# Edge offsets of a graph kernel: a second copy in bf16, stored in reading order

## The chip, the cores and the metric

The kernel runs on one core of one Trainium2 chip. The metric is the device time of one execution in microseconds, as the median of several runs. The engines are TensorE (PE, with its weight loads as PEld), VectorE (DVE), ScalarE (ACT), GpSimd (POOL) and SyncE (SP, which here only issues DMAs).

## What is computed

A graph of N = 6250 nodes with 128 features and E = 200000 edges, sorted by destination. First one attention layer (GAT) with 4 heads, a residual and a layer norm; then three message-passing layers with a gate per edge, and a last residual and layer norm.

```
xh = (x @ W).reshape(-1, H, C)                      # GAT
alpha = leaky_relu((xh[dst]*a_i).sum(-1) + (xh[src]*a_j).sum(-1), 0.2)
ex = exp(alpha - segment_max(alpha, dst)[dst])
out = segment_sum(xh[src] * ex / segment_sum(ex, dst)[dst], dst)
...
for l in range(3):                                  # message passing
    hk = relu(concat([h[dst], h[src]]) @ linA_w[l].T + linA_b[l])
    w = sigmoid(hk @ linB_w[l].T + linB_b[l])
    prop = segment_sum(w * h[src], dst)
    emb = relu(concat([h, prop]) @ lin_w[l].T + lin_b[l])
```

## The kernel before

The edges are worked in NG = 392 groups of GE = 512. Within a group, edge p*4 + t (T = 4) lies in partition p, column t. Since the edges are sorted, the destinations of a group nearly always lie in a window of W = 32 nodes that begins at the group's `base`; the rare further windows have a loop of their own (`extra_windows`), which finds nothing to do with these inputs.

For each group four things are made ready:
- **The source rows.** GpSimd gathers one table row of 1 KB for each edge, with four indirect DMAs of 128 rows for a group (`gather`, L572, the issue is L579). The tables are `gat_rows` for GAT and `mp_rows` for a layer. The target `G` has U = 8 slots; from the ninth group on a gather waits until the group eight earlier has been used up (`R` in GAT, `agg` in a layer). The row numbers are copied to `idx` by ScalarE (L654) some four groups ahead.
- **The window.** SyncE loads the offsets of the group's 512 edges from `REL` in DRAM, broadcast to 128 partitions (GAT, L477) or 96 (a layer, L532), into a ring of four slots `relbc`, and the window's own rows (`sm` or `awin`). An offset is destination minus base.
- **The one-hot `sel`,** edges in partitions, 32 nodes in columns (L965).
- **The transposed one-hot `selT`,** nodes in partitions, 512 edges in columns, in bf16. `make_selT` (L968, the operation is L969) compares the broadcast offsets with the partition's node number. The offsets lie in edge order (p, t); TensorE takes 128 edges of one t as weights, so the result is written in the order (t, p): the read runs through, the write goes from one t to the next at a stride of 128 elements of 2 bytes. It is used as weights in L1523 (GAT) and L1636 (a layer).

Each engine works through a software pipeline written out by hand: on VectorE in the order `gat_order` or `mp_order`, where the first number is how many groups a stage lags. Per step of a layer these are hidden (L1341, one group behind, waits for the gathered rows), the sum into `acc` (L1371), the transposed one-hot (L969), logits (L1352), the weighted one-hot (L1360) and `sel` (L965). In GAT the transposed one-hot comes between the maximum of the group before (L996) and the product `R` (L1105, the gathered rows by the exponentials, both in SBUF). Two short casts (L1013, L1022) round to bf16 there. `rhs` (L1035) is VectorE's last result before TensorE's L1523. Loops run over turns of eight groups; VectorE loads the bases of a turn into registers at its start (L1147).

Ahead of it all, VectorE prepares the lists: L884 makes the offsets `relF` (98 partitions of 2048), L887 casts the sources, L893 copies TensorE's transposes of both lists, and up to L914 follow small steps. The semaphore `prep` counts these. SyncE stores `REL` (L443) after L884; GpSimd fills `acc` (L569) when all are done and `REL` is stored, since the lists lie in the same memory. Then come the GAT table (SyncE L455) and the first gathers.

Of the kernel before, what the change touches and what calls it, by code (L numbers as in the profile page):

```python
# [16 lines left out]
BF16 = mybir.dt.bfloat16  # L17
ALU = mybir.AluOpType
# [3 lines left out]
T = 4  # L22
GE = P * T
W = 32
# [21 lines left out]
PREP_SRC = PREP_REL + 1  # L46
# [44 lines left out]
def gnn_kernel(nc, x, src, dst, W0, att, linA_w, linA_b, linB_w, linB_b, lin_w, lin_b, gamma, beta, final_w, final_b,  # L91
# [20 lines left out]
    PADDST = 16 * N  # L112

# [5 lines left out]
    REL = nc.dram_tensor("rel_dst", (NG, GE), F32, kind="Internal").ap()  # L119
    MORE = nc.dram_tensor("more_windows", (1, NG), I32, kind="Internal").ap()  # L120
    BASE = nc.dram_tensor("window_base", (1, NG), I32, kind="Internal").ap()

    with ExitStack() as ctx:
# [18 lines left out]
        relF = mh[0:QP, 0:QW]  # L142

# [19 lines left out]
        relbc = ring[:, 0:4, :]  # L163
# [99 lines left out]
        rel_stored = sem("rel_stored")  # L263
        base_stored = sem("base_stored")
# [145 lines left out]
        def _(sp):  # L410
# [32 lines left out]
            sp.dma_start(REL.rearrange("(q c) e -> q (c e)", c=CQ), relF).then_inc(rel_stored, 16)  # L443
            sp.wait_ge(base_stored, 16)
# [24 lines left out]
            sp.wait_ge(rel_stored, 16)  # L469
            sp.wait_ge(pads_stored, 32)  # L470
            sp.wait_ge(si_out, 16 * NT)

            def gat_window(k0, off):
                base = sp.value_load(base_sb[0:1, bass.ds(k0 + off, 1)], min_val=0, max_val=N - 1)
                if reached(k0, off, 4):
                    sp.wait_ge(gat["rhs"], k0 + (off - 3))
                sp.dma_start(relbc[:, off % 4, :], REL[bass.ds(k0 + off, 1), :].rearrange("o e -> (o e)")  # L477
                             .partition_broadcast(P)).then_inc(win_in[off % 4], 16)
                sp.dma_start(sm[:, off % 4, 0, 0:1], SI[bass.ds(base * H, W * H), :]).then_inc(win_in[off % 4], 16)
# [7 lines left out]
            with extra_windows(sp, 0) as at:  # L487
                sp.wait_ge(x_free, at.w + (at.q + 1))
                sp.sem_inc(waited, 1)
                sp.dma_start(relbc[:, 0, :], REL[bass.ds(at.g, 1), :].rearrange("o e -> (o e)")  # L490
                             .partition_broadcast(P)).then_inc(x_win, 16)
                sp.dma_start(sm[:, 0, 0, 0:1], SI[bass.ds(at.node * H, W * H), :]).then_inc(x_win, 16)
# [12 lines left out]
            with sp.Fori(0, L) as l:  # L505
# [22 lines left out]
                def window(k0, off):  # L528
# [3 lines left out]
                    sp.dma_start(relbc[0:S * W, off % 4, :], REL[bass.ds(k0 + off, 1), :].rearrange("o e -> (o e)")  # L532
# [11 lines left out]
                with extra_windows(sp, l + 1) as at:  # L544
                    sp.wait_ge(x_free, at.w + (at.q + 1))
                    sp.sem_inc(waited, 1)
                    sp.dma_start(relbc[0:S * W, 0, :], REL[bass.ds(at.g, 1), :].rearrange("o e -> (o e)")
                                 .partition_broadcast(S * W)).then_inc(x_win, 16)
                    sp.dma_start(awin[:, 0, :],
                                 A3[bass.ds(at.node, W), :].rearrange("n (s d) -> (n s) d", s=S)).then_inc(x_win, 16)  # L550
# [12 lines left out]
        def _(pool):  # L563
# [4 lines left out]
            pool.wait_ge(rel_stored, 16)  # L568
            nc.gpsimd.memset(acc[:, :, :], 0.0).then_inc(acc_cleared, 1)  # L569
# [269 lines left out]
        def _(dve):  # L839
# [46 lines left out]
            assert done[0] == PREP_REL  # L886
            then(v.tensor_copy(srcF, srcI))  # L887
# [80 lines left out]
            def make_selT(k0, off, tile, rows, node, made):  # L968
                v.tensor_scalar(tile[0:rows, off % 4, :].rearrange("n (t p) -> n p t", t=T),  # L969
                                relbc[0:rows, off % 4, :].rearrange("n (p t) -> n p t", t=T),  # L970
                                node, None, ALU.is_equal).then_inc(made, 1)
# [182 lines left out]
            def make_extra_sel(at, tile, rows, node, selT_done, sel_done, window):  # L1154
# [8 lines left out]
                                relbc[0:rows, 0, :].rearrange("n (p t) -> n p t", t=T),  # L1163
# [558 lines left out]
```

## Time and profile before

| what | value |
|---|---|
| median of 3 runs | 9366.73 us (9366.05 to 9370.35) |
| span of the profiled execution | 9351.7 us |
| GpSimd busy | 6739.1 us (72%) |
| VectorE busy | 6023.4 us (64%) |
| TensorE busy | 4974.9 us (53%) |
| ScalarE busy | 1410.9 us (15%) |
| gathers in GAT, L579 | 1568, 1779.5 us |
| gathers in the layers, L579 | 4704, 4920.1 us |
| transposed one-hot, L969 | 1568, 2178.9 us |
| DMA engines, share of the span | gathers 30.2%, queue of SyncE and ScalarE 15.6% |

The profile is of one execution, whose own time is not listed among the runs; its span is from the first to the last instruction. A busy time is the sum of an engine's instructions without register and semaphore work. A busy engine need not be the one that sets the time: that is read from the chain that ended last and from what each instruction waited for. TensorE is granted half of its full clock nearly throughout (0.515 on the mean).

### The profile page before, as it was taken

How to read it: one execution, taken by the hardware profiler on the slowest of the kernel's cores; microseconds unless marked ns; L12 is line 12 of the kernel's file. 1: busy time of each engine (PE TensorE's matmuls, PEld its weight loads, DVE VectorE, ACT ScalarE, POOL GpSimd, SP SyncE). 2: the span in 40 equal slices, each digit the busy share in tenths (PEclk: the TensorE clock that was granted, in tenths of full speed). 3: DMA queues.
4: the chain of work that ended last, by engine and by line, in shares of the span. 5: the costliest groups of instructions: out<-in, count | busy, mean ns of one | idle time of the engine just before them, and what ended most of it. 6: DMA issues, size and time to landing. Idle time of an engine off the chain costs nothing.

```text
span 9351.7 us, 148690 instructions
## 1 busy us (share of the span) xinstructions
PE 4974.9 (53%) x27078; PEld 4220.6 (45%) x27079; DVE 6023.4 (64%) x26793; ACT 1410.9 (15%) x5406; POOL 6739.1 (72%) x6331
## 2 busy tenths in 40 slices
PE   2777777777744444444454444444445444444445
PEld 1666666666633333333343333333334333333334
DVE  4888888888856555555556555655555555555656
ACT  1222222222410000000020000000002000000002
POOL 1777777777457777777746777777773777777774
PEclk7555555555555555555565555555556555555555
DMA  2444444444344444444434444444443444444443
GB/s 81 138 137 138 138 138 137 137 138 138 92 137 138 138 138 138 138 138 137 138 109 133 139 138 138 139 138 138 138 135 108 139 137 138 139 138 139 138 139 100
DMA packets 752005, 1241.72 MB, mean 133 GB/s; under 512 B 323315, under 2 KB 387641, under 8 KB 751419
## 3 DMA queue, kind: packets, MB, share of 16 engines
q0 software_dynamic: 301056, 822.48, 30.2%
q1 hardware_dynamic: 444380, 413.53, 15.6%
q10 hardware_dynamic: 6275, 3.20, 0.1%
q14 instruction: 283, 2.32, 0.1%
q8 instruction: 11, 0.18, 0.0%
HBM read 1194.48 MB, written 44.13 MB: 132 GB/s over the span
## 4 chain that ended last, share of the span: by engine, by line
POOL 54%; issue 24%; DMA 6%; DVE 5%; PE 5%; SPq 2%; DVEq 1%; POOLq 1%; ACT 0%; ACTq 0%
POOL G L579 54%; DMA G<-mp_rows,idx 3%; DMA G<-gat_rows,idx 2%; PE ps L1646 2%; DVE junk L1352 1%; SPq L520 1%; PE ps L1551 1%; SPq L513 1%; DMA gat_rows<-ring 1%; DMA mp_rows<-acc 0%; PE ps L1511 0%; DVEq L957 0%; SPq L414 0%; DMA mp_dst_rows<-acc 0%; PE ps L1676 0%
## 5 line engine op out<-in xcount | busy, mean ns | idle before, releaser
L579 POOL DMA_INDIRECT G<-mp_rows,idx x4704 | 4920.1, 1046 | 1810.7 <-issue 1391.1
L1646 PE MATMUL ps<-selw,G 128*128 128x32 f32 x9408 | 2222.2, 400 | 468.8 <-DVE selw L1360 462.9
L1646 PEld LDWEIGHTS ps<-selw,G 128*128 128x128 f32 x9408 | 2093.9, 327 | 751.2 <-issue 652.3
L1341 DVE TENSOR_TENSOR pen<-ps,G 128x512 f32<-128x512 f32 x1176 | 813.1, 691 | 2502.2 <-DMA G<-mp_rows,idx 2500.0
L1636 PE MATMUL ps<-awin,ring 96*128 96x128 bf16 x4704 | 714.5, 307 | 2986.2 <-DVE ring L969 2986.2
L969 DVE TENSOR_SCALAR ring<-ring,pF 96x512 bf16<-96x512 f32 (+1 forms) x1568 | 2178.9, 1390 | 2.5 <-DMA sm<-gat_si 2.1
L579 POOL DMA_INDIRECT G<-gat_rows,idx x1568 | 1779.5, 1135 | 552.7 <-issue 526.5
L1636 PEld LDWEIGHTS ps<-awin,ring 96*128 96x128 bf16 x4704 | 404.2, 130 | 3142.9 <-DVE ring L969 3142.9
L1352 DVE SCALAR_TENSOR_TENSOR junk<-pen,cur 128x128 f32<-128x128 f32 x4704 | 1282.3, 328 | 0.1
L787 ACT ACTIVATE gate<-logit,cur 128x4 f32<-128x4 f32 x1176 | 349.6, 297 | 5870.5 <-DVE junk L1352 5263.8
L1551 PE MATMUL ps<-sel,weighted 128*128 128x32 f32 x3136 | 750.7, 404 | 0.0
L1551 PEld LDWEIGHTS ps<-sel,weighted 128*128 128x128 f32 x3136 | 698.0, 327 | 25.3
L1511 PE MATMUL ps<-ident,G 128*128 128x128 f32 x1568 | 428.7, 429 | 345.3 <-DMA G<-gat_rows,idx 344.9
L666 ACT ACTIVATE pen<-ring,negbig 128x512 f32<-128x512 bf16 x392 | 282.9, 722 | 1518.8 <-DVE ring L969 1518.8
L965 DVE TENSOR_TENSOR sel<-iotaF,rel_all 128x128 f32<-128x128 f32 x1568 | 449.6, 287 | 13.0 <-issue 11.6
L996 DVE CUSTOM_DVE_ANT_0 junk<-ps,pen 128x512 f32<-128x512 f32 x392 | 268.7, 685 | 291.0 <-issue 240.9
L1511 PEld LDWEIGHTS ps<-ident,G 128*128 128x128 f32 x1568 | 280.6, 217 | 363.6 <-issue 236.7
L1352 DVE DVE_READ_ACCUMULATOR junk<-pen,cur 128x1 f32 x4704 | 378.8, 81 | 0.0
L1360 DVE TENSOR_TENSOR selw<-sel,gate 128x128 f32<-128x128 f32 x1176 | 334.6, 285 | 0.2
L654 ACT COPY idx<-idx_all 128x4 int32 (+1 forms) x1572 | 284.3, 182 | 40.7 <-issue 40.6
L1105 DVE TENSOR_TENSOR weighted<-G,weighted 128x512 f32<-128x512 f32 x392 | 270.9, 691 | 0.0
L1523 PE MATMUL ps<-rhs,ring 128*128 128x24 bf16 x1568 | 106.6, 184 | 281.4 <-DVE rhs L1035 281.3
(176 smaller groups left out, 5146.1 us busy)
## 6 DMA issues: line engine op xcount, KB each, us to landing
ring<-rel_dst SPq DMA_DIRECT2D x1176, 192.0 KB
ring<-rel_dst SPq DMA_DIRECT2D x392, 256.0 KB
G<-mp_rows,idx POOLq DMA_INDIRECT x4704
awin<-mp_dst_rows SPq DMA_DIRECT2D x1176, 24.0 KB
G<-gat_rows,idx POOLq DMA_INDIRECT x1568
mp_rows<-acc SPq DMA_DIRECT2D x30, 625.0 KB
mp_dst_rows<-acc SPq DMA_DIRECT2D x30, 468.8 KB
sm<-gat_si SPq DMA_DIRECT2D x392, 0.5 KB
```

The source lines that it names most:

```text
L579: pool.indirect_dma_start(out=G[:, u, width * t:width * (t + 1)], out_offset=None, in_=table, in_offset=bass.IndirectOffsetOnAxis(ap=idx[: ...
L654: nc.scalar.copy(idx[:, T * (off % U):T * (off % U) + T], idx_all[:, bass.ds(k0 * T + off * T, T)]).then_inc(idx_ready, 1)
L787: nc.scalar.activation(gate[:, off % 4, :], logit[:, off % 4, :], ACT.Sigmoid, bias=cur[:, C_BB:C_BB + 1]).then_inc(done["gate"], 1)
L965: v.tensor_tensor(sel[:, off % U, :].rearrange("p (t n) -> p t n", t=T), iotaW, rel4, ALU.is_equal).then_inc(made, 1)
L969: v.tensor_scalar(tile[0:rows, off % 4, :].rearrange("n (t p) -> n p t", t=T), relbc[0:rows, off % 4, :].rearrange("n (p t) -> n p t", t=T ...
L1341: v.tensor_tensor(pen[:, off % 2, :].rearrange("p (t c) -> p t c", t=T), PS[off % 2][:, :].rearrange("p (t c) -> p t c", t=T), Grows[:, of ...
L1352: v.scalar_tensor_tensor(junk[:, P * t:P * t + P], pen[:, off % 2, P * t:P * t + P], 0.0, cur[:, C_B:C_B + D], ALU.max, ALU.mult, accum_ou ...
L1360: v.tensor_tensor(selw[:, off % 4, :].rearrange("p (t n) -> p t n", t=T), sel[:, off % U, :].rearrange("p (t n) -> p t n", t=T), gate[:, o ...
L1511: i = tr(PS[off % 2][:, P * t:P * t + P], Grows[:, off % U, t, D:2 * D], ident[:, :])
L1551: i = mm(PS[4 + b][:, 0:W], R[:, b, D * t:D * t + D], sel[:, off % U, W * t:W * t + W], start=(t == 0), stop=(t == T - 1))
L1636: i = mm(PS[off % 2][:, D * t:D * t + D], selT16[0:S * W, off % 4, P * t:P * t + P], awin[:, off % 4, :], start=True, stop=True)
L1646: i = mm(PS[2 + off % 2][:, 0:W], Grows[:, off % U, t, 0:D], selw[:, off % 4, W * t:W * t + W], start=(t == 0), stop=(t == T - 1))
```

## The change

The offsets are stored a second time, in `REL16`, as bf16 and in the order (t, p). One VectorE operation on the 98x2048 offsets makes them, between the making of `relF` and the cast of the sources; it also limits them to 255, which changes no comparison with 0 to 31 and keeps what is stored a whole number that bf16 holds exactly. SyncE stores them, and waits for that store before the first window; so does GpSimd before it fills `acc`. The window loads of both stages read `REL16`. `make_selT` compares with unit stride on both sides, bf16 in and out. The loops over further windows go on with `REL` in fp32.

```diff
+    NONE16 = 255.0
+    REL16 = nc.dram_tensor("rel_dst16", (NG, GE), BF16, kind="Internal").ap()
+        rel16 = acc[0:QP, 0, 2 * QW:3 * QW].bitcast(BF16)[:, 0:QW]
-        relbc = ring[:, 0:4, :]
+        relbc = ring[:, 0, :]
+        relbc16 = ring[:, 0:4, :].bitcast(BF16)[:, :, 0:GE]
...
             sp.dma_start(REL.rearrange("(q c) e -> q (c e)", c=CQ), relF).then_inc(rel_stored, 16)
+            sp.wait_ge(prep, PREP_REL16)
+            sp.dma_start(REL16.rearrange("(q c) e -> q (c e)", c=CQ), rel16).then_inc(rel16_stored, 16)
...
+            sp.wait_ge(rel16_stored, 16)
...
-                sp.dma_start(relbc[:, off % 4, :], REL[bass.ds(k0 + off, 1), :].rearrange("o e -> (o e)")
+                sp.dma_start(relbc16[:, off % 4, :], REL16[bass.ds(k0 + off, 1), :].rearrange("o e -> (o e)")
...
-                    sp.dma_start(relbc[0:S * W, off % 4, :], REL[bass.ds(k0 + off, 1), :].rearrange("o e -> (o e)")
+                    sp.dma_start(relbc16[0:S * W, off % 4, :], REL16[bass.ds(k0 + off, 1), :].rearrange("o e -> (o e)")
...
             pool.wait_ge(rel_stored, 16)
+            pool.wait_ge(rel16_stored, 16)
...
+            then(v.tensor_single_scalar(rel16.rearrange("q (c t p) -> q c p t", c=CQ, t=T),
+                                        relF.rearrange("q (c p t) -> q c p t", c=CQ, t=T), NONE16, ALU.min))
+            assert done[0] == PREP_REL16
             then(v.tensor_copy(srcF, srcI))
...
             def make_selT(k0, off, tile, rows, node, made):
-                v.tensor_scalar(tile[0:rows, off % 4, :].rearrange("n (t p) -> n p t", t=T),
-                                relbc[0:rows, off % 4, :].rearrange("n (p t) -> n p t", t=T),
-                                node, None, ALU.is_equal).then_inc(made, 1)
+                v.tensor_scalar(tile[0:rows, off % 4, :], relbc16[0:rows, off % 4, :], node, None,
+                                ALU.is_equal).then_inc(made, 1)
```

No instruction changes its place; one is added on VectorE and one DMA on SyncE. VectorE's preparation before, where the names are output<-input:

```order
L884 TENSOR_TENSOR mh<-acc,baseF 98x2048
L887 CAST acc<-acc 98x2048
L893 COPY rel_all<-ps 128x4x98 x4
L893 CAST idx_all<-ps 128x4x98 x4
L895 COPY idx_all<-idx_all 128x16
```

The same place in the changed kernel:

```order
L894 TENSOR_TENSOR mh<-acc,baseF 98x2048
L897 TENSOR_SCALAR acc<-mh 98x4x128x4
L900 CAST acc<-acc 98x2048
L906 COPY rel_all<-ps 128x4x98 x4
L906 CAST idx_all<-ps 128x4x98 x4
L908 COPY idx_all<-idx_all 128x16
```

The new operation (L897) stands ahead of the cast of the sources, so all that follows on VectorE comes after it.

## Rows read from the trace of the kernel before

**Rows 1.** the page's part 4, shares of the chain that ended last, by line
```profile
POOL G L579 54%; DMA G<-mp_rows,idx 3%; DMA G<-gat_rows,idx 2%; PE ps L1646 2%; DVE junk L1352 1%; SPq L520 1%; PE ps L1551 1%; SPq L513 1%; DMA gat_rows<-ring 1%; DMA mp_rows<-acc 0%; PE ps L1511 0%; DVEq L957 0%; SPq L414 0%; DMA mp_dst_rows<-acc 0%; PE ps L1676 0%
```

**Rows 2.** L579 by stretch: length, busy us (x count), granted clock, DMA share, GB/s
```profile
196.50:2453.40 2256.90, 1779.48 (x1568) 0.50 0.49 138
2605.00:4761.80 2156.80, 1643.69 (x1568) 0.50 0.48 138
4864.20:7016.70 2152.50, 1639.14 (x1568) 0.50 0.48 138
7117.70:9268.30 2150.60, 1637.18 (x1568) 0.50 0.48 138
sum 8716.80, POOL 6699.49; mean POOL 1674.87
```

**Rows 3.** single lines: ns min/median/max, first to last start, forms; then its wait
```profile
L969 DVE TENSOR_SCALAR ring<-ring,pF x1568: 1347/1357/1604, 203.7 to 9265.5; 96x512 bf16<-96x512 f32 x147, 128x512 bf16<-128x512 f32 x49
...
  DMA sm<-gat_si: 2.1, 1
...
L579 POOL DMA_INDIRECT G<-mp_rows,idx x4704: 942/947/1943, 2605.0 to 9267.3; - x196
...
L1299 DVE TENSOR_SCALAR ring<-mh x150: 210/221/440, 2573.0 to 7148.4; 128x125 f32 x90, 128x125 f32<-128x125 f32 x60
```

**Rows 4.** timeline, message passing: start us, us, engine, line, [idle before]
```profile
5500.60 0.69 DVE L1341 TENSOR_TENSOR pen<-ps,G 128x512 f32<-128x512 f32 x1 [2.97 <-DMA G<-mp_rows,idx]
5500.85 1.93 POOL L579 DMA_INDIRECT G<-mp_rows,idx  x1 [0.30 <-issue]
...
5501.30 1.35 DVE L969 TENSOR_SCALAR ring<-ring,pF 96x512 bf16<-96x512 f32 x1
...
5506.83 0.95 POOL L579 DMA_INDIRECT G<-mp_rows,idx  x1 [0.30 <-issue]
...
5507.58 1.36 DVE L969 TENSOR_SCALAR ring<-ring,pF 96x512 bf16<-96x512 f32 x1
```

**Rows 5.** timeline, GAT: short VectorE operations beside gathers
```profile
644.35 0.69 DVE L1105 TENSOR_TENSOR weighted<-G,weighted 128x512 f32<-128x512 f32 x1
644.55 1.32 POOL L579 DMA_INDIRECT G<-gat_rows,idx  x1 [0.30 <-issue]
...
1223.55 1.05 POOL L579 DMA_INDIRECT G<-gat_rows,idx  x1 [0.30 <-issue]
...
1223.78 0.17 DVE L1022 CAST sm<-sm 128x2 bf16<-128x2 f32 x1
```

**Rows 6.** timeline, GpSimd: first gather without L969, first with, last with, last without
```profile
196.46 1.10 POOL L579 DMA_INDIRECT G<-gat_rows,idx  x1 [75.30 <-issue]
...
203.01 0.95 POOL L579 DMA_INDIRECT G<-gat_rows,idx  x1 [0.30 <-issue]
...
9265.55 1.46 POOL L579 DMA_INDIRECT G<-mp_rows,idx  x1 [0.30 <-issue]
9267.31 0.95 POOL L579 DMA_INDIRECT G<-mp_rows,idx  x1 [0.30 <-issue]
```

**Rows 7.** timeline, GAT: VectorE's pause, then TensorE from group to group
```profile
1220.30 0.69 DVE L996 CUSTOM_DVE_ANT_0 junk<-ps,pen 128x512 f32<-128x512 f32 x1 [5.82 <-issue]
...
1224.99 0.26 PE L1523 MATMUL ps<-rhs,ring 128*128 128x24 bf16 x4 [3.86 <-DVE rhs L1035]
...
1229.68 0.26 PE L1523 MATMUL ps<-rhs,ring 128*128 128x24 bf16 x4 [0.48 <-DVE rhs L1035]
...
1234.24 0.26 PE L1523 MATMUL ps<-rhs,ring 128*128 128x24 bf16 x4 [0.35 <-DVE rhs L1035]
```

**Rows 8.** timeline, start: VectorE's cast, its next copy, GpSimd's fill
```profile
82.77 1.23 DVE L887 CAST acc<-acc 98x2048 f32<-98x2048 int32 x1
90.48 3.42 DVE L893 COPY rel_all<-ps 128x392 f32<-128x392 f32 x4 [6.48 <-PE ps L1481]
...
104.98 10.76 POOL L569 MEMSET acc<- 128x12800 f32 x1 [103.73 <-DVE moreI L914]
```

More of the change, by code:

```diff
@@ L45 @@
 PREP_REL = PREP_CONST + 5
-PREP_SRC = PREP_REL + 1
+PREP_REL16 = PREP_REL + 1
+PREP_SRC = PREP_REL16 + 1
 PREP_IDX = PREP_SRC + 2 * T + 1
@@ L263, in gnn_kernel @@
         rel_stored = sem("rel_stored")
+        rel16_stored = sem("rel16_stored")
         base_stored = sem("base_stored")
@@ L489, in _ @@
                 sp.sem_inc(waited, 1)
-                sp.dma_start(relbc[:, 0, :], REL[bass.ds(at.g, 1), :].rearrange("o e -> (o e)")
+                sp.dma_start(relbc, REL[bass.ds(at.g, 1), :].rearrange("o e -> (o e)")
                              .partition_broadcast(P)).then_inc(x_win, 16)
@@ L546, in _ @@
                     sp.sem_inc(waited, 1)
-                    sp.dma_start(relbc[0:S * W, 0, :], REL[bass.ds(at.g, 1), :].rearrange("o e -> (o e)")
+                    sp.dma_start(relbc[0:S * W, :], REL[bass.ds(at.g, 1), :].rearrange("o e -> (o e)")
                                  .partition_broadcast(S * W)).then_inc(x_win, 16)
@@ L1162, in make_extra_sel @@
                 v.tensor_scalar(tile[0:rows, 0, :].rearrange("n (t p) -> n p t", t=T),
-                                relbc[0:rows, 0, :].rearrange("n (p t) -> n p t", t=T),
+                                relbc[0:rows, :].rearrange("n (p t) -> n p t", t=T),
                                 shift[0:rows, 0:1], node, ALU.subtract, ALU.is_equal).then_inc(selT_done, 1)
```

## The prediction

> **What bounds the kernel now.** I read the views in this order. The chain that ended last comes first: more than half of it is GpSimd issuing gathers on one line [rows 1]. Then that line alone, in the four stretches in which gathers run, the GAT pass and three message-passing layers: each stretch has 1568 of them, and together the stretches are 8716.8 us of the 9351.7 us span [rows 2]. So outside the stretches lie only 634.9 us, and the time of the kernel is above all the number of gathers times the pitch of one. The reader is to see in the timeline what a pitch is: a gather of 0.95 us, then 0.30 us of issue, with no wait for a buffer or a result [rows 4]. Nothing on GpSimd stands between two gathers, so only the length of a gather can change its pace.
>
> That length varies. In the message-passing layers its median is 947 ns, its minimum 942 ns, its maximum 1943 ns [rows 3]. 6272 gathers of 0.947 us would be 5939.6 us; the profile has 6699.5 [rows 2]. The excess is 759.9 us.
>
> Where does it come from? Laying GpSimd beside VectorE shows it. In the message-passing stage a gather that starts at 5500.85 lasts 1.93 us; the transposed one-hot (L969) starts 0.45 us after it and ends at 5502.65, and the gather ends 0.13 us later. One turn on, the same VectorE operation starts 0.75 us into a gather, and that gather takes its usual 0.95 us [rows 4]. So GpSimd stands still in the middle of a gather until L969 has ended. I did this for all 6272: 2213 gathers have L969 running somewhere in their span, and they hold 721.3 us of the excess; the other 4059 hold 38.7 us. The first and the last gather of the two sets are in [rows 6]. The 38.7 us belong to other VectorE work: a gather with a two-input product at its start takes 1.32 us [rows 5].
>
> The Trainium skill (SBUF — State Buffer, "SBUF: two separate sides") has the mechanism: VectorE and GpSimd share a pair of ports, and a VectorE operation in a two-port mode keeps GpSimd from writing descriptors; the next section of that page has it blocked until about 115 ns after the operation's end. The 0.13 us above agrees. The page also speaks against this change: a bf16 operation of unit stride is in its faster two-port mode, so it would still lock.
>
> **The change part by part.** *The one-hot itself.* There are 1176 + 392 = 1568 of them, each 1.36 us now for 512 elements [rows 3]. That is 2.65 ns an element, while a two-input fp32 product over 512 elements needs 0.69 us [rows 5]; what L969 has and the product has not is an output scattered over 2-byte elements at a stride of 128. The change makes input and output bf16 and contiguous. The trace has no such operation. The bounds are the nearest rows: 0.22 us for a one-input fp32 operation over 125 elements [rows 3] from below, and the 0.69 us of the product from above. I take 0.3 us: the product has two inputs, and the form is nearer to the one-input row. The Trainium skill (VectorE: DVE Perf Modes, "Side-by-side") would give (150 + 8 + 128) cycles at 0.96 GHz, an estimate of 0.30 us for the new form; for the old one it would allow two elements a cycle, some 0.43 us, and the measured 1.36 us decides against that.
>
> VectorE itself gains nothing for the time by this, since it waits for gathers. What counts is how much of the 721.3 us stays. What a short one does, the trace shows with a cast of 0.17 us (L1022), by the same engine and with one input: of 390 casts placed clear of L969, 44 started 0.2 to 0.3 us after a gather and cost it 0.10 us, as at 1223.55 [rows 5]; 53 cost some 0.01 us and the others nothing. That is 0.01 us each. A 0.3 us operation covers the sensitive places (the start of the gather, which the product at 644.35 hits, and about 0.25 us in) twice as often, and for about 0.15 us longer. In GAT, L969 starts 0.1 to 0.3 us after a gather's start in 130 of 392 cases, at some 0.15 to 0.2 us each: 22 us. In message passing 1130 of 1176 start later than 0.45 us after a gather's start, where that gather takes no harm [rows 4]; 536 of these start in the last 0.3 us before the next gather and can reach into its start. Half of them at some 0.06 us are 15 us. Together 37 us stay, between 0 (all fall free) and 130 us (0.25 us for a third of 1568). The term is -721 + 37 = **-684 us**.
>
> *The loads.* The broadcast of the offsets moves half the bytes, 1568 times. Nobody waits for these loads: the only wait for the window is a single one, at the first group [rows 3]. Zero; the cover is that a load is issued about three groups ahead, and if it were gone the load would still be shorter than before.
>
> *The preparation.* A 98x2048 operation is added on VectorE between L884 and L887, in the scattered form on its output. At L969's 2.65 ns an element it takes 5.4 us; contiguous it would be the 1.23 us of the cast behind it [rows 8]. That cast now starts at 82.77 and ends at 84.00; the next instruction starts at 90.48, after 6.48 us of idleness until TensorE's transposes [rows 8]. With 5.4 us more the cast ends at 89.4, still before 90.48. Taken at 0, at most 1 us. Behind the new wait on SyncE stand the load of the bases and the stores of the pads, and on GpSimd the fill of `acc`, which starts at 104.98 after 103.7 us of idleness that the end of VectorE's preparation sets [rows 8]; the store issued at about 88 has 16 us to land. Zero.
>
> *What is late next.* At 1.25 us a gather, a group is 5.0 us of GpSimd. In message passing VectorE has 3 us to spare, spent waiting for gathers [rows 4]. In GAT less is to spare: when gathers are there in time, TensorE takes 4.69 and 4.56 us from one group to the next, of which 0.48 and 0.35 us are waiting for VectorE, so 4.2 us of its own [rows 7]. And once in a turn of eight groups VectorE stands for 5.8 us, which TensorE sees as a wait of 3.9 us [rows 7]. The turn is now 2256.9 / 49 = 46.1 us. As they are, those two would allow 8 x 4.6 + 5.8 = 42.6 us; with L969 1 us shorter the waits of 0.35 to 0.48 us go, and it is 8 x 4.2 + 3.9 = 37.5. GpSimd needs 8 x 4 x 1.25 = 40.0. So GpSimd stays the bound, by 2.5 us of 40, and what is late next is again the gather.
>
> **Sum.** The profiled execution has a span of 9351.7 us and becomes 9351.7 - 684 = 8667.7 us. The median of the runs, 9366.7, lies 15.0 us above the span, for what is around it: 9366.7 - 684 = **8683 us**.
>
> **Rivals.**
> *In proportion (10%).* The blocking may not fall away below a certain length but shrink with it. Now each L969 costs 721 / 1568 = 0.46 us of a possible 1.36 + 0.12 = 1.48, or 31%. At the same share an operation of 0.3 us costs 0.13 us and one of 0.69 us costs 0.25 us: 204 or 394 us stay in place of 37, so 8850 to 9040 us. For it: short operations do get hit [rows 5]. Against it: the cast, which would have to cost 0.09 us and costs 0.01. The Trainium skill (SBUF — State Buffer, "Who interferes with whom") is on this rival's side: a two-port operation, the fastest mode included, blocks GpSimd fully until it is done.
> *GAT is paced by TensorE and VectorE (6%).* If the wait of TensorE does not shrink, the turn can't go below 42.6 us, 2.6 us over 40, 49 times: 127 us, less the 22 us of blocking in GAT that are hidden then, so 8683 + 105 = 8788 us. For it: the pause of 5.8 us is not touched by the change. Against it: L969 stands in the very loop (sum, L969, rhs, TensorE) that sets the 4.6 us.
> *The change doesn't do what it says (4%).* If the length of L969 comes from the comparison with a per-partition operand and not from the scattered output, it stays at 1.36 us and so does the time, 9367.
> *Slower (2%).* bf16 input is what costs: the operation grows instead of shrinking. It decides from the present 1.36 us on. At 2.0 us the blocked share rises in proportion to 2.12 / 1.48, 721 becomes 1033 us, and the time is about 9680. No VectorE row here reads bf16 in bulk, so it can't be excluded; that the write is the scattered side speaks against it.
> *Everything falls free.* With 0 instead of 37 it is 8646, within the forecast; if the other 39 us went too, 8607.
>
> **How the numbers follow.** The forecast has 76%. Its own range is 8646 to 8776, from 0 and 130 us of blocking that stays, with 15 us more below for a part of the other 39. Proportion has 10%, pace 6, unchanged 4, slower 2, and below 8630 lie 2. The range 8630 to 8800 takes in the forecast and the pace of GAT, 82% together. Faster by over 0.2% (19 us, about what a measurement of this kernel can tell from no change): 0.94; within: 0.04; slower: 0.02.
>
> **What would show it.** Right: the one-hot near 0.3 us; gathers per stretch near 1568 x 0.95 us = 1490 us busy; all four gather stretches near 2010 us (GAT 2257 - 270 + 22, the others 2153 - 150 + 5), where now GAT is 100 us longer than the others; the maximum of a gather well below 1.9 us; the first VectorE copy of the transposed offsets still near 90.5. Wrong: gathers whose 0.30 us of issue becomes a wait for a buffer (another bound), a mean gather above 1.0 us (in proportion), or a one-hot above 0.7 us.

## The result and the profile after

The changed kernel takes **9884.42 us** (median of 5 runs, 9801.19 to 9893.52), the kernel before 9366.73 us beside it: a ratio of 1.0533, interval 1.0499 to 1.0566. It is 5.3% slower where I had forecast 7.3% faster, and it lies outside my range. The profiled execution, the fastest of the five, took 9801.19 us with a span of 9799.4 us.

GpSimd's gathers again hold most of the chain that ended last, 60% instead of 54% [rows 1]. Part 4 of the page, shares by line:

```profile
POOL G L589 60%; DMA G<-gat_rows,idx 2%; PE ps L1563 2%; SPq L529 1%; PE ps L1523 1%; ACTq L641 1%; DMA gat_rows<-ring 1%; SPq L522 1%; PE ps L1560 1%; PE ps L1550 0%; DMA mp_rows<-acc 0%; POOLq L586 0%; DVE weighted L1117 0%; PE ps L1658 0%; DMA mp_dst_rows<-acc 0%
```

The gathers (now L589) by stretch, GAT first, then the three layers: length, busy time (x count), granted clock, DMA share, GB/s. It answers to [rows 2]:

```profile
198.00:2241.80 2043.80, 1566.34 (x1568) 0.50 0.48 127
2393.60:4773.30 2379.70, 1869.92 (x1568) 0.50 0.39 109
4875.00:7235.00 2360.00, 1849.80 (x1568) 0.50 0.39 109
7338.30:9715.60 2377.30, 1867.19 (x1568) 0.50 0.38 109
sum 9160.80, POOL 7153.25; mean POOL 1788.31
```

The GAT stretch lost 213 us, and each layer gained 208 to 227. Outside the stretches lie 9799.4 - 9160.8 = 638.6 us, against 634.9 before, so nearly all of the change is in the stretches. I call **excess** what the 1568 gathers of a stretch take beyond 1568 x 0.947 = 1484.9 us. In GAT it fell from 295 to 81 us; in the layers it rose from 159, 154 and 152 to 385, 365 and 382 us.

Single lines of the changed kernel (ns minimum/median/maximum, first to last start, forms), beside [rows 3]: the one-hot, the gathers, the logit operation.

```profile
L982 DVE TENSOR_SCALAR ring<-ring,pF x1568: 339/343/586, 206.2 to 9713.2; 96x512 bf16<-96x512 bf16 x147, 128x512 bf16<-128x512 bf16 x49
...
L589 POOL DMA_INDIRECT G<-mp_rows,idx x4704: 940/946/2329, 2393.6 to 9714.5; - x196
L589 POOL DMA_INDIRECT G<-gat_rows,idx x1568: 942/946/1467, 198.0 to 2240.9; - x196
...
L1364 DVE SCALAR_TENSOR_TENSOR junk<-pen,cur x4704: 270/282/293, 2460.3 to 9721.3; 128x128 f32<-128x128 f32 x196
```

The one-hot fell from 1357 to 343 ns, as the change says. The median gather is as before. But the longest gather of the layers grew from 1.94 to 2.33 us while the operation I blamed for the long ones shrank to a quarter. The timeline shows why. It answers to [rows 4] (start us, us, engine, line, [idle before]):

```profile
5687.94 0.34 DVE L982 TENSOR_SCALAR ring<-ring,pF 96x512 bf16<-96x512 bf16 x1
5688.07 2.29 POOL L589 DMA_INDIRECT G<-mp_rows,idx  x1 [0.30 <-issue]
5688.20 0.28 DVE L1364 SCALAR_TENSOR_TENSOR junk<-pen,cur 128x128 f32<-128x128 f32 x1
...
5688.84 0.28 DVE L1364 SCALAR_TENSOR_TENSOR junk<-pen,cur 128x128 f32<-128x128 f32 x1
...
5689.05 0.28 DVE L1372 TENSOR_TENSOR selw<-sel,gate 128x128 f32<-128x128 f32 x1
...
5689.25 0.28 DVE L978 TENSOR_TENSOR sel<-iotaF,rel_all 128x128 f32<-128x128 f32 x1
...
5690.66 0.95 POOL L589 DMA_INDIRECT G<-mp_rows,idx  x1 [0.30 <-issue]
...
5693.60 0.69 DVE L1353 TENSOR_TENSOR pen<-ps,G 128x512 f32<-128x512 f32 x1 [4.07 <-DMA G<-mp_rows,idx]
```

Behind the one-hot stand six operations in a row, each 0.21 us behind the last: four logit operations, the weighted one-hot, the one-hot by edges. Every one reads two inputs from SBUF. I call them **the run**. The last ends at 5689.25 + 0.28 = 5689.53, and the gather ends at 5688.07 + 2.29 = 5690.36, 0.83 us later. Of the layers' 4704 gathers, 1097 end 0.82 us after the end of such an L978, and they hold 1133 us. VectorE then waits for gathers, 4230.0 us in all against 2500.0 before (waits of VectorE, L1353; longest wait last):

```profile
DVE pen L1353 <- DMA G<-mp_rows,idx: 4230.0, 1149, 5.1
```

In the kernel before the same six operations stood behind the one-hot, but no gather was held for the length of the run. Of the gathers that were held there in the layers, 55 end 0.12 us behind the one-hot's end, as in [rows 4]. The other 1109 start 0.09 to 0.78 us into the one-hot and end 0.30 to 0.34 us behind its end. One of them, from the timeline before:

```profile
5495.12 1.35 DVE L969 TENSOR_SCALAR ring<-ring,pF 96x512 bf16<-96x512 f32 x1
5495.41 1.37 POOL L579 DMA_INDIRECT G<-mp_rows,idx  x1 [0.30 <-issue]
...
5496.08 0.50 DVE L1352 SCALAR_TENSOR_TENSOR junk<-pen,cur 128x128 f32<-128x128 f32 x1
```

The one-hot ends at 5496.47 and the gather at 5496.78. If 0.82 us follow the release here as in the changed kernel, this gather was let go at 5495.96, 0.12 us ahead of the first logit operation. That is an estimate.

### The profile page after: what moved, and what is told of

It reads as the page before. It is cut to its first block, busy times and chain, and to the rows that moved or that the text cites. A ratio compares the mean times of both kernels' runs of the same rounds, so it can differ in the third digit from the quotient of the medians.

```text
span 9799.4 us, 148692 instructions
## 1 busy us (share of the span) xinstructions
PE 4945.8 (50%) x27078; PEld 4213.5 (43%) x27079; DVE 4664.4 (48%) x26794; ACT 1412.8 (14%) x5406; POOL 7192.8 (73%) x6331
## 4 chain that ended last, share of the span: by engine, by line
POOL 60%; issue 21%; PE 6%; DVE 4%; DMA 4%; SPq 2%; POOLq 1%; ACTq 1%; DVEq 1%; ACT 0%
POOL G L589 60%; DMA G<-gat_rows,idx 2%; PE ps L1563 2%; SPq L529 1%; PE ps L1523 1%; ACTq L641 1%; DMA gat_rows<-ring 1%; SPq L522 1%; PE ps L1560 1%; PE ps L1550 0%; DMA mp_rows<-acc 0%; POOLq L586 0%; DVE weighted L1117 0%; PE ps L1658 0%; DMA mp_dst_rows<-acc 0%
## 5 line engine op out<-in xcount | busy, mean ns | idle before, releaser
L589 POOL DMA_INDIRECT G<-mp_rows,idx x4704 | 5587.0, 1188 | 1802.5 <-issue 1429.7
L1353 DVE TENSOR_TENSOR pen<-ps,G 128x512 f32<-128x512 f32 x1176 | 813.3, 692 | 4235.3 <-DMA G<-mp_rows,idx 4230.0
L589 POOL DMA_INDIRECT G<-gat_rows,idx x1568 | 1566.4, 999 | 554.1 <-issue 535.3
L1364 DVE SCALAR_TENSOR_TENSOR junk<-pen,cur 128x128 f32<-128x128 f32 x4704 | 1079.7, 282 | 0.1
L982 DVE TENSOR_SCALAR ring<-ring,pF 96x512 bf16<-96x512 bf16 (+1 forms) x1568 | 559.7, 357 | 2.4 <-DMA sm<-gat_si 2.0
L978 DVE TENSOR_TENSOR sel<-iotaF,rel_all 128x128 f32<-128x128 f32 x1568 | 443.4, 283 | 3.6
L664 ACT COPY idx<-idx_all 128x4 int32 (+1 forms) x1572 | 284.5, 182 | 42.1 <-issue 41.7
L692 ACT ACTIVATE weighted<-al 128x512 f32<-128x512 f32 x392 | 246.5, 629 | 104.0 <-DVE al L1088 101.8
```

Source lines behind the costliest of these rows:

```text
L589: pool.indirect_dma_start(out=G[:, u, width * t:width * (t + 1)], out_offset=None, in_=table, in_offset=bass.IndirectOffsetOnAxis(ap=idx[: ...
L664: nc.scalar.copy(idx[:, T * (off % U):T * (off % U) + T], idx_all[:, bass.ds(k0 * T + off * T, T)]).then_inc(idx_ready, 1)
L978: v.tensor_tensor(sel[:, off % U, :].rearrange("p (t n) -> p t n", t=T), iotaW, rel4, ALU.is_equal).then_inc(made, 1)
L982: v.tensor_scalar(tile[0:rows, off % 4, :], relbc16[0:rows, off % 4, :], node, None, ALU.is_equal).then_inc(made, 1)
L1353: v.tensor_tensor(pen[:, off % 2, :].rearrange("p (t c) -> p t c", t=T), PS[off % 2][:, :].rearrange("p (t c) -> p t c", t=T), Grows[:, of ...
L1364: v.scalar_tensor_tensor(junk[:, P * t:P * t + P], pen[:, off % 2, P * t:P * t + P], 0.0, cur[:, C_B:C_B + D], ALU.max, ALU.mult, accum_ou ...
```

## The experiments

Twelve kernels first tell where the loss is and what makes it. "Layers' excess" is the sum over the three layers (465 us before, 1132 after). The column "in the run" counts gathers that start 0.6 to 0.9 us after the start of the first logit operation, so in the middle of the run, with their median and longest duration in us. The ratio is to the kernel before on the same chip.

| kernel | us | ratio (interval) | layers' excess | in the run |
|---|---|---|---|---|
| before | 9366.73 | 1 | 465 | 55: 0.95, 0.95 |
| changed | 9884.42 | 1.0533 (1.0499 to 1.0566) | 1132 | 197: 1.35, 1.54 |
| gat_only | 9145.64 | 0.9774 (0.9758 to 0.9791) | 470 | 67: 0.95, 0.95 |
| layers_psum | 8664.02 | 0.9262 (0.9247 to 0.9278) | -2 | 248: 0.95, 0.96 |
| before_psum | 9346.31 | 0.9989 (0.9979 to 0.9999) | 462 | 55: 0.95, 0.96 |
| logits_psum | 8780.43 | 0.938 (0.9365 to 0.9396) | 107 | 319: 1.26, 1.39 |
| onehot_last | 8754.98 | 0.9353 (0.9338 to 0.9369) | 77 | 66: 0.95, 1.07 |
| layers_fill_half | 8862.56 | 0.9479 (0.9463 to 0.9495) | 196 | none |
| fill_tiny | 9964.07 | 1.063 (1.0578 to 1.0683) | 1321 | 100: 1.34, 1.54 |
| fp32_unit | 8856.2 | 0.9462 (0.9447 to 0.9478) | 185 | 109: 0.95, 1.07 |
| fp32_unit_small16 | 8817.84 | 0.9416 (0.94 to 0.9431) | 145 | 165: 0.96, 1.07 |
| small32_between | 8709.75 | 0.9298 (0.9283 to 0.9314) | 45 | 168: 0.95, 1.07 |
| drained | 8714.93 | 0.9307 (0.9292 to 0.9323) | 44 | 78: 0.95, 1.07 |
| sum_between | 9312.22 | 0.9943 (0.9919 to 0.9966) | 677 | 147: 1.32, 1.53 |

The last column falls into two classes. In one, a gather that starts in the middle of the run is held for at most 0.13 us; in the other it is always held until the run's end (in logits_psum, whose run is only the last two operations, from a start at 0.76 us on). I call these the **open** and the **shut** run.

### Where the loss is

**gat_only**: the new form in the GAT pass alone; the layers keep the fp32 broadcast and the scattered compare.

```
-                    make_selT(k0, off, selT16, S * W, pF[0:S * W, 5:6], done["selT"])
+                    v.tensor_scalar(selT16[0:S * W, off % 4, :].rearrange("n (t p) -> n p t", t=T),
+                                    relbc32[0:S * W, off % 4, :].rearrange("n (p t) -> n p t", t=T),
+                                    pF[0:S * W, 5:6], None, ALU.is_equal).then_inc(done["selT"], 1)
```

> The new transposed one-hot and its bf16 loads in the GAT pass alone; the three layers keep the fp32 load and the scattered compare, as before the change. Theory A (in the layers the fast one-hot lets VectorE's run of two-input operations, logits, weighted one-hot and one-hot, start where it holds up a gather's read): the GAT stretch stays at 2044 us as in the changed kernel (2257 before), the layers return to 2151 to 2157 us each, and the time is 9367 - 213 = 9154 us. Theory B (transfers: the bf16 loads in 1 KB pieces make gathers land later) and theory C (the bf16 one-hot itself locks GpSimd) expect the same of the layers, but should have made GAT slower too; if either holds, GAT in this run is longer than 2100 us.

Measured: 9145.64 us, a GAT stretch of 2042.2 us, layers of 2151.9, 2157.5 and 2155.9 us, as before. So the GAT half of the change is a gain of 2.3%, and the whole loss is made in the layers.

**layers_psum**: the changed kernel with one input of each of the six operations in PSUM (the hidden rows, the one-hot by edges and the row of numbers that it compares with). **before_psum**: the same in the kernel before.

```
-                    v.tensor_tensor(pen[:, off % 2, :].rearrange("p (t c) -> p t c", t=T),
+                    v.tensor_tensor(PS[4 + off % 2][:, :].rearrange("p (t c) -> p t c", t=T),
...
-                                    sel[:, off % U, :].rearrange("p (t n) -> p t n", t=T),
+                                    sel_ps[:, off % 4, :].rearrange("p (t n) -> p t n", t=T),
...
+                v.tensor_copy(PS[7][:, 0:W], iotaF[:, 0:W]).then_inc(l_iota, 1)
```

> The changed kernel, and in the layers each of the six operations of VectorE's run has at most one input in SBUF: the hidden values, the one-hot and the counting row lie in PSUM. Nothing else moves: loads and bf16 one-hot as in the changed kernel. Theory A: no gather in the layers is held up, each layer stretch is 1568 x 1.25 + 38 = about 2000 us instead of 2360 to 2380, and the time is 9884 - 3 x 372 = about 8770 us, or 8685 by the profiled run's 9801. Theories B and C: no change, 9800 to 9900 us.

> The kernel before, with the same three things in PSUM in the layers. Theory A: the run of two-input operations costs the kernel before next to nothing (38.7 us of excess outside the scattered one-hot), the scattered one-hot goes on holding up gathers by some 150 us a layer, so 9350 to 9380 us. If the run also mattered before, it is below 9300 us.

Measured: 8664.02 and 9346.31 us. Gathers of layers_psum, single lines and a stretch of its timeline:

```profile
L591 POOL DMA_INDIRECT G<-mp_rows,idx x4704: 940/946/1068, 2388.7 to 8576.9; - x196
L591 POOL DMA_INDIRECT G<-gat_rows,idx x1568: 942/946/1447, 197.3 to 2236.0; - x196
```

```profile
4752.91 0.34 DVE L984 TENSOR_SCALAR ring<-ring,pF 96x512 bf16<-96x512 bf16 x1
4753.01 1.06 POOL L591 DMA_INDIRECT G<-mp_rows,idx  x1 [0.30 <-issue]
4753.17 0.28 DVE L1369 SCALAR_TENSOR_TENSOR junk<-ps,cur 128x128 f32<-128x128 f32 x1
```

The gather starts 0.16 us ahead of the first logit operation, where it took 2.3 us in the changed kernel; here it takes 1.06, and ends 0.82 us behind the one-hot. The operations are as long as before (0.28 us); one input of each has moved, and with it the place to which two results are written. With that the excess of 1132 us is gone: the run of two-input operations is what makes the loss. The bf16 loads and the bf16 one-hot are those of the changed kernel, so neither makes it alone (theories B and C of the expectation). This shows three more things. The bf16 one-hot by itself costs the layers next to nothing, not even the 15 us that I had given it: it holds a gather for 0.12 us at most. In the kernel before, the same edit brings 0.1%, so there the run cost next to nothing. And this kernel is the fastest of all, 7.4% ahead of the kernel before.

**logits_psum** has the first of these three edits alone (the hidden rows in PSUM, the last two operations as they were).

> The changed kernel with only the hidden values in PSUM: the four logit operations behind the one-hot have one SBUF input each; the weighted one-hot and the one-hot by edges (0.28 us each) keep two. Theory A1: a run of 0.5 us is left, which holds a gather for at most 0.5 + 0.82 - 0.95 = 0.4 us: 0.1 to 0.2 us a group, 8780 to 8900. Theory A2: nothing follows the one-hot that could inherit its hold: close to the 8664 of the run with all three in PSUM, 8665 to 8720.

Measured: 8780.43 us. The long gathers that are left end 0.82 us behind L978's end, and they start 0.76 to 1.01 us after the first logit operation: the last two operations of the run still shut a gather out, for as long as they last.

### What makes the run shut

**onehot_last**: the one-hot after the run instead of ahead of it.

```
-                mp_order = ((1, mp_hidden), (4, mp_E), (0, mp_selT), (1, mp_logit), (2, mp_C), (0, mp_sel))
+                mp_order = ((1, mp_hidden), (4, mp_E), (1, mp_logit), (2, mp_C), (0, mp_sel), (0, mp_selT))
```

> The changed kernel with the layers' order on VectorE turned: the one-hot last, behind the two-input operations (hidden, sum, logits, weighted one-hot, one-hot by edges, transposed one-hot). Same operations, nothing added. Theory A1 (the run of two-input operations alone keeps GpSimd's read waiting): the run is where it was or 0.26 us earlier, gathers go on being held, and the layers' stretches stay above 2250 us, the time above 9500. Theory A2 (GpSimd is shut out only where the run follows directly on the two-port one-hot, whose hold it inherits; in the run with the fill, gathers that started 0 to 0.4 us after the first logit operation took 0.95 to 1.04 us, while in the changed kernel those near it took 2.1 to 2.3): stretches of about 2000 to 2050 us, the time 8680 to 8830.

Measured: 8754.98 us, the longest gather of the layers 1073 ns, as theory A2 expected. The same instructions in another order cost 77 us instead of 1132.

**layers_fill_half** and **fill_tiny** put a fill of 512 and of 8 columns between the one-hot and the run.

```
+                    v.memset(ex.rearrange("p a c -> p (a c)")[:, 0:512], 0.0).then_inc(filled, 1)
```

> The changed kernel with a fill of 512 elements on VectorE (no input, some 0.45 us) between the one-hot and the logits in the layers, so that the run of two-input operations starts that much later against the gathers. VectorE has more work. Theory A: the gather that was held up from its first tenths of a microsecond is past them, and the next one meets the run 0.65 us in: some 0.56 us lost a group instead of 0.97, 1176 x 0.4 = 480 us less, about 9400 us. Theories B and C, and any theory of VectorE's amount of work: no gain, 9880 us or more.

> The changed kernel with a fill of 8 elements (some 0.06 us) between the one-hot and the logits in the layers. It moves the run by less than 0.1 us. Theory A1, or any theory of where the run lies against the gathers: 9700 us or more, since the gathers that are held start up to 0.25 us before the run. Theory A2: one operation that uses no shared port breaks the hold, and the time is 8700 to 8900, as with the long fill (8863) or better.

Measured: 8862.56 and 9964.07 us, on opposite sides of 9884. The first is far below the 9400 us that theory A gave it; the second is where theory A1 had it, and not theory A2. With 512 columns held gathers end 0.82 us behind the end of the *first* logit operation; with 8 columns behind that of the run's last one, as in the changed kernel. One turn of each, layers_fill_half first:

```profile
5504.26 0.48 DVE L1389 MEMSET weighted<- 128x512 f32 x1
...
5504.34 1.37 POOL L590 DMA_INDIRECT G<-mp_rows,idx  x1 [0.30 <-issue]
5504.66 0.23 DVE L1365 SCALAR_TENSOR_TENSOR junk<-pen,cur 128x128 f32<-128x128 f32 x1
```

```profile
5505.86 2.19 POOL L590 DMA_INDIRECT G<-mp_rows,idx  x1 [0.30 <-issue]
5505.91 0.28 DVE L1365 SCALAR_TENSOR_TENSOR junk<-pen,cur 128x128 f32<-128x128 f32 x1
5505.92 0.07 DVE L1389 MEMSET weighted<- 128x8 f32 x1
```

In the first, 5504.34 + 1.37 = 5505.71, and the logit operation ends at 5504.89. The small fill is recorded beside the logit operation, not ahead of it, so by the record it separated nothing.

**fp32_unit**: the second copy of the offsets in reading order, but as fp32: unit stride without bf16 input. **fp32_unit_small16**: the same, with a 64-element bf16 compare behind the one-hot. **small32_between**: the changed kernel with a 64-element fp32 compare there.

```
-    REL16 = nc.dram_tensor("rel_dst16", (NG, GE), BF16, kind="Internal").ap()
+    REL16 = nc.dram_tensor("rel_dst16", (NG, GE), F32, kind="Internal").ap()
...
+                    v.tensor_scalar(scrap[:, :], ident[:, 0:64], 3.0, None, ALU.is_equal).then_inc(filled, 1)
```

> The changed kernel with the second copy in fp32: reading order and unit stride on both sides kept, loads of 2 KB a partition as before the change. Theories A1 and A2: the operation stays short (some 0.45 us) and in a two-port mode, so the layers lose about as in the changed kernel: 9600 to 9950 us. Theory B (the loss comes from the bf16 loads in 1 KB pieces): the loss is gone, below 9200. Theory C (the 16-bit mode itself is what locks): below 9200 as well.

> The kernel with the fp32 copy in reading order (8856 us), with a small bf16 compare of 64 elements between its one-hot and the logits in the layers. Theory S, and theory H as far as it needs the 16-bit form: the loss of the changed kernel comes back, above 9500 us. Theory P (only the place of the run against the gathers counts; the small operation moves it by 0.1 to 0.2 us): 8850 to 9000.

> The changed kernel with a small fp32 compare of 64 elements (two-port, not 16-bit) between the bf16 one-hot and the logits in the layers. Theories S and H with the 16-bit form as cause: what stands directly before the run is now an fp32 operation, as in the fp32 kernel, so about 8850 to 9000 us. If any two-port operation before the run does it, or if the state lasts, 9700 or more.

Measured: 8856.2, 8817.84 and 8709.75 us. All three runs are open. So the 9600 to 9950 us that both A1 and A2 gave fp32_unit didn't come, nor the 9500 and more that theories S and H gave fp32_unit_small16: there a bf16 compare of 64 elements stands directly ahead of the run and doesn't shut it. Whether one of 512 elements behind the fp32 one-hot would, no run shows. small32_between still loads bf16, so the size of the loads doesn't shut the run either. A turn of fp32_unit:

```profile
5507.82 0.48 DVE L982 TENSOR_SCALAR ring<-ring,pF 96x512 bf16<-96x512 f32 x1
5508.02 1.30 POOL L589 DMA_INDIRECT G<-mp_rows,idx  x1 [0.30 <-issue]
5508.21 0.28 DVE L1364 SCALAR_TENSOR_TENSOR junk<-pen,cur 128x128 f32<-128x128 f32 x1
```

This gather starts 0.19 us ahead of the first logit operation and ends at 5509.32, 0.83 us behind that operation's end. Gathers that start at the same place in both kernels, 0.09 to 0.11 us ahead of that operation, take 1.19 to 1.22 us here and 2.24 to 2.27 us in the changed kernel. So where a gather starts isn't what decides it: with an fp32 input of the one-hot the run is open, with bf16 shut. The unit stride alone, with the fp32 broadcast of full size, makes the kernel 5.4% *faster* than before; the bf16 input turns that into a loss.

**drained**: VectorE waits for the end of its own one-hot before the first logit operation.

```
+                def mp_drained(k0, off):
+                    dve.wait_ge(mp["selT"], km + k0 + (off + 1))
+                    dve.sem_inc(waited, 1)
```

> The changed kernel, but in the layers VectorE waits for the end of the transposed one-hot before it starts the logits, so the two don't overlap any more (now the first logit operation starts 0.26 us after a one-hot of 0.34 us). Theory H (hold handed over: GpSimd is shut out of the whole run because the first logit operation is already there when the two-port one-hot ends): the hold is broken, 8650 to 8900 us. Theory S (a 16-bit two-port operation leaves VectorE in a state in which back-to-back two-input operations don't let GpSimd in, whatever the gap): as the changed kernel, 9700 to 10000.

Measured: 8714.93 us with no other edit, as theory H expected, from a pause of 0.26 us in most groups, up to 0.33 us as in this one:

```profile
5503.48 0.34 DVE L982 TENSOR_SCALAR ring<-ring,pF 96x512 bf16<-96x512 bf16 x1
5503.58 1.06 POOL L589 DMA_INDIRECT G<-mp_rows,idx  x1 [0.30 <-issue]
...
5504.15 0.29 DVE L1364 SCALAR_TENSOR_TENSOR junk<-pen,cur 128x128 f32<-128x128 f32 x1 [0.33 <-DVE ring L982]
...
5504.95 0.95 POOL L589 DMA_INDIRECT G<-mp_rows,idx  x1 [0.30 <-issue]
```

The second gather starts 0.80 us into the run and isn't held: the pause doesn't only let one gather in, the whole run behind it is open.

**sum_between**: the one-hot ahead of the sum (L1383, 0.18 us) instead of behind it.

> The changed kernel with one exchange in the layers' order: the transposed one-hot before the sum into acc, so that the sum (one SBUF input, one PSUM input, 0.18 us) stands between the one-hot and the logits. Theory H: the sum takes no shared read port, the hold is not handed over, 8650 to 8900 us. Theory S (with logits that read PSUM in between, the two-input pair behind them still held gathers for their length): the loss stays, above 9600.

Measured: 9312.22 us. Neither expectation: the runs are shut, as the table's last column shows, but fewer gathers fall into them. The sum between the bf16 one-hot and the run doesn't open it.

### Three more

By then my theory was a hand-over (H): the hold passes from the bf16 one-hot to the operation directly behind it. sum_between spoke against it, so three more kernels test it. **first_op_psum** has the linear layer's row in PSUM for the first logit operation only, **rest_ops_psum** for the other three only; **sum_between_drained** is sum_between with a wait for the sum's end ahead of the run.

```
-                                               cur[:, C_B:C_B + D], ALU.max, ALU.mult,
+                                               PS[7][:, 0:D] if t == 0 else cur[:, C_B:C_B + D],
...
+                    dve.wait_ge(mp["acc"], km + k0 + (off + 1))
```

> In the layers the first of the four logit operations takes its second input (the linear layer's row) from a copy in PSUM, the other three, the weighted one-hot and the one-hot by edges still have two inputs in SBUF: a run of five such operations instead of six, and it no longer starts directly behind the bf16 one-hot. Theory H (the hold is handed over from the bf16 one-hot to the first two-input operation behind it, and then lasts for the run): 8700 to 8800 us, as where VectorE paused between the two (8714.93 us). Theory L (a gather that starts at a certain place just ahead of the logit operations waits out the whole run wherever that run begins): the five operations end as late as the six, so 9600 to 9900 us.

> The reverse: the first logit operation keeps two inputs in SBUF directly behind the bf16 one-hot, the other three take the row from a copy in PSUM, and the weighted one-hot and the one-hot by edges keep two inputs in SBUF. Theories H and L: the hold ends with the first logit operation, 0.82 us behind its end, so a long gather is about 1.0 us shorter than the 2.2 to 2.3 us of the changed kernel: 8750 to 9000 us. If the operations behind the first hold a gather whatever they read: over 9500 us.

> The one-hot stands before the sum, as in sum_between (9312.22 us), and VectorE then waits for the end of the sum before it starts the logit operations, a pause of some 0.3 us. Theory P (what lets GpSimd in is a moment in which VectorE executes nothing ahead of the run): 8700 to 8850 us. Theory N (the run holds a gather by where in it the gather starts, pause or not): 9200 to 9400 us.

Measured: 10721.54, 10752.04 and 10757.17 us, all far outside what was expected. But the kernel before took 10908.11 us in that job, where it had 9355.86 to 9366.73 in the others; the ratios are 0.9836 (0.9812 to 0.986), 0.986 (0.9836 to 0.9885) and 0.9869 (0.9845 to 0.9893). In first_op_psum the gathers (L590, what ended GpSimd's idle time ahead of them) wait for what cost the changed kernel less (the first 117.7 us) or nothing (the second):

```profile
  ACT idx L665: 1055.1, 203
  remote: 869.1, 279
```

What slowed that job isn't known, and the times don't bear on the theories. How long single gathers are held can still be read, since what isn't held takes 0.947 us in that job too (the median of first_op_psum). Layers' excess is 264, 116 and 81 us. A turn of first_op_psum:

```profile
5001.05 0.34 DVE L983 TENSOR_SCALAR ring<-ring,pF 96x512 bf16<-96x512 bf16 x1
5001.31 0.28 DVE L1368 SCALAR_TENSOR_TENSOR junk<-pen,ps 128x128 f32<-128x128 f32 x1
5001.52 0.28 DVE L1368 SCALAR_TENSOR_TENSOR junk<-pen,cur 128x128 f32<-128x128 f32 x1
5001.56 1.90 POOL L590 DMA_INDIRECT G<-mp_rows,idx  x1 [0.30 <-issue]
...
5002.36 0.28 DVE L979 TENSOR_TENSOR sel<-iotaF,rel_all 128x128 f32<-128x128 f32 x1
```

The gather ends at 5003.46, 0.82 us behind the end of L979. A logit operation that reads PSUM stands between the one-hot and the first operation with two SBUF inputs, and still the run is shut: the hand-over falls. In rest_ops_psum gathers at the first operation end 0.82 us behind its end and those at the last two 0.82 us behind L979's; each stretch of such operations holds a gather by itself. Only an input of the logit operations moves to PSUM in this kernel, no result, so with them it is the read that holds. In sum_between_drained 955 gathers start 0.6 to 0.9 us into the run and none takes more than 1.062 us, against 1.53 in sum_between. So far theory P holds: a pause opens the run, in both orders. It isn't the only thing that does, as small32_between shows.

**What stays open.** A run ahead of which stands the bf16 one-hot is shut, and it stays so across the sum or a PSUM-reading operation in between. It is open after a pause (0.26 to 0.33 us), after the 64-element fp32 compare, after the fill of 512 columns, and after an fp32 one-hot in either form, also with a 64-element bf16 compare behind it. In onehot_last, which is open too, VectorE's wait for the gathers, the hidden rows and the sum stand between the one-hot and the next run. What these have in common, and why the state then lasts for the whole run, no run shows.

## Why the prediction was wrong

**What bounds the kernel: right.** Gathers set the pace before and after, at 0.305 us of issue between two.

**The one-hot's length: right.** 0.3 us forecast, 0.343 measured. The bf16 input doesn't make it longer, and the rival "doesn't do what it says" is out.

**GAT: right, somewhat too good.** I forecast 2009 us for the stretch; it is 2043.8. Its excess is 81 us. What is left is mostly one thing, the product of [rows 5], whose gathers end 0.82 us behind it. Timeline of the changed kernel:

```profile
1220.25 0.69 DVE L1117 TENSOR_TENSOR weighted<-G,weighted 128x512 f32<-128x512 f32 x1
1220.45 1.32 POOL L589 DMA_INDIRECT G<-gat_rows,idx  x1 [0.30 <-issue]
```

They are 202 and hold 75 us, where before they were 47 and 17 us: the shorter chain of VectorE moved the product onto the starts of more gathers. At 2043.8 / 49 = 41.7 us a turn the stretch is below the 42.6 us that the rival of the pace gave as its floor, so that rival is out too.

**Preparation and loads: right.** The added operation takes 5.36 us (5.4 forecast), hides ahead of TensorE's transposes, and the next copy starts at 90.47, against 90.48 in [rows 8]:

```profile
82.92 5.36 DVE L897 TENSOR_SCALAR acc<-mh 98x2048 bf16<-98x2048 f32 x1
...
90.47 3.41 DVE L906 COPY rel_all<-ps 128x392 f32<-128x392 f32 x4 [0.92 <-PE ps L1493]
```

**The step that failed is the 38.7 us.** I put 721.3 us on gathers with L969 in their span and 38.7 us on "other VectorE work", and carried the second term over unchanged, also as the bound of what could be lost ("15 us more below"). For the layers this gave 3 x (150 - 5) = 435 us less. In the profiled executions the layers' stretches went from 6459.9 to 7117.0 us, 657 more. The blocked time of the other operations was small in the kernel before not because they hardly block, but because of where gathers met them and in which state: a gather that met L969 ended at most 0.34 us behind its end and wasn't held again by the run, and none started in the first 0.8 us of a run. The meeting is no accident of single groups. VectorE starts a step when the gathered rows have landed, and from there (the start of L1341, now L1353) the run comes after 1.67 us before and after 0.97 us now, where the next gather starts after 0.86 us (all medians). The shorter one-hot brought the run 0.7 us forward, onto the gathers' starts. In the changed kernel 776 gathers start in the 0.18 us ahead of the run, where the kernel before has none, and these and 15 more take over 2.07 us. I had even shown the mechanism, a two-input product at a gather's start that costs 0.37 us [rows 5], and then counted only what it cost so far. What I took for a property of each operation was one of the order and of the neighbours. My reading of L969 was narrow too: the hold in a gather's middle that I showed from [rows 4] is that of the 55 gathers with 43 us, while the 1109 that start during L969 hold 409 of the layers' 465 us.

**The rival in proportion** named the right mechanism, a hold until the operation is done, but applied it to the one-hot alone, as I applied the Trainium skill's rule to it. The Trainium skill (SBUF — State Buffer, "Who interferes with whom") also has the rule that a VectorE instruction with two SBUF inputs contends with GpSimd's reads of SBUF, and six such instructions stood in [rows 4]'s gap between the one-hot and the next turn. layers_psum agrees with that rule, 1132 us to nothing. That six of them can hold like one of 1.33 us is what the timeline at 5688.07 shows.

**The slower rival (2%)** priced a longer one-hot, which didn't come. A rival of the right kind had its price in the trace of the kernel before: the run lasts 1.33 us, 0.82 us of the gather follow its end; a gather that starts with it would take 2.15 us, 1.2 us too long, and 1176 of these would be 1411 us. The point from which it decides is whether the gathers meet the run.

**15.0 us around the span** was wrong as well, and small: here 9801.19 - 9799.4 = 1.8 us. If as little lies around it in the kernel before, its profiled execution took 9353.5 us and was simply shorter than the median run.

## What to carry to other kernels

When an operation that holds another engine is made shorter, what stands behind it on its engine comes forward and meets the other engine's work in places where it never was: count what *every* neighbour would cost if it were met, not what it costs now. Where GpSimd issues gathers all the time, give VectorE's two-input operations one input in PSUM (8664 against 9884 us here), or at the least look for runs of them behind a short bf16 operation and break these with a pause (8715 us). And try the parts of a change singly: the same edit was worth -2.3% in one stage and +7.6 points in the other.

## What the runs showed of the hardware

- A gather of 128 rows takes 0.947 us, of which 0.82 us follow its release: gathers held at their start by a unit-stride bf16 one-hot, a two-input product or the run end 0.82 us behind the end of what held them. Those that start 0.09 to 0.78 us into the scattered one-hot of the kernel before end 0.30 to 0.34 us behind its end, those stopped later 0.12 us behind it.
- Six 0.28 us operations with two SBUF inputs, 0.21 us apart, hold a gather like one operation of 1.33 us (2.29 us in all) when a 512-element bf16 compare of unit stride went ahead; when VectorE had paused for 0.26 us in between, no gather that started in them took more than 1.07 us.
- A compare of 512 elements takes 1.357 us scattered, 0.477 us with unit stride and fp32 input, 0.343 us with bf16 input. The slower of the last two makes the faster kernel (8856 against 9884 us).
- One input in PSUM instead of SBUF costs those operations nothing: 0.28 us in both.
